# A two-layer transformer block on one core: another order of layer 1's steps

## What is computed

```python
# layer 0: full attention, 16 heads of 8; then 16 experts, one per token, and a shared one
h = layernorm(x) * (1 + ca) + sa
q, k, v = h @ Wq.T + bq, h @ Wk.T + bk, h @ Wv.T + bv
x = x + ga * (softmax(q @ k.T / sqrt(8)) @ v @ Wo.T + bo)
h = layernorm(x) * (1 + cb) + sb
scores = sigmoid(top1(h @ router_w.T))
gate, up = split(routed_in @ gate_up_proj[expert])
routed = (up * silu(gate)) @ down_proj[expert]
shared = silu(h @ shared_gate_w.T) * (h @ shared_up_w.T) @ shared_down_w.T
x = x + gb * (routed + shared)
# layer 1: causal attention, 8 query heads of 16 on one key and value head; then a token mix
h = layernorm(x) * (1 + ca) + sa
x = x + ga * (softmax(causal(q @ k.T * 128 ** -0.5)) @ v @ Wp + bp)
h = layernorm(x) * (1 + cb) + sb
r = sigmoid(mix_r(h) @ W_r.T); kk = square(relu(mix_k(h) @ W_k.T))
x = x + gb * r * (kk @ W_v.T)
```

## Time and profile before

| | us |
|---|---|
| median of 3 runs | 1134.35 (1130.43 to 1134.98) |
| the profiled execution | 1135.12 |
| its span, first to last instruction | 1133.3 |
| PE busy in the span | 1029.5 (91%) |
| DVE, ACT, POOL busy | 895.8, 821.1, 173.1 |
| mean granted TensorE clock | 0.952 |

### The profile page before, as it was taken

How to read it: one execution, slowest core, us unless ns; L and a number is a source line. 1 busy time by engine, 2 the same in 40 slices (tenths; PEclk the granted TensorE clock), 3 DMA queues, 4 the chain that set the end, 5 groups by cost and what they waited for, 6 DMA issues and landing times.

```text
span 1133.3 us, 22270 instructions
## 1 busy us (share of the span) xinstructions
PE 1029.5 (91%) x8778; PEld 356.0 (31%) x8778; DVE 895.8 (79%) x1131; ACT 821.1 (72%) x1585; POOL 173.1 (15%) x312
## 2 busy tenths in 40 slices
PE   4889999999999999999988998899978888798997
PEld 2332222222222222222222443343434453233314
DVE  5999999999999999999996776666756568587603
ACT  3239999998999989999875775467644555466675
POOL 4433200003000030000232002310221013000101
PEclk9569999999999999999998999899989999899987
DMA  3450511000000000000006221042003211200000
GB/s 108 128 142 7 136 30 29 2 2 2 2 2 2 2 2 1 2 2 2 2 19 188 61 72 36 13 95 49 2 1 112 82 52 30 36 10 2 11 1 10
DMA packets 47694, 42.08 MB, mean 37 GB/s; under 512 B 6534, under 2 KB 45798, under 8 KB 47590
## 3 DMA queue, kind: packets, MB, share of 16 engines
q1 hardware_dynamic: 45190, 35.17, 12.3%
q0 software_dynamic: 1824, 5.25, 1.6%
q10 hardware_dynamic: 576, 0.23, 0.1%
...
## 4 chain that ended last, share of the span: by engine, by line
PE 68%; DVE 17%; ACT 6%; issue 4%; DMA 2%; POOL 1%; SPq 1%; another core or an unknown queue 0%; DVEq 0%; POOLq 0%; ACTq 0%
PE O L936 24%; PE T L907 13%; DVE mx L1202 9%; PE S L866 8%; PE S L873 4%; ACT PT L1446 3%; PE T L916 3%; PE S L1047 2%; PE S L1015 1%; PE T L1055 1%; PE S L916 1%; PE T L945 1%; PE S L1005 1%; DVE Vf L1262 1%; DVE Vf L1266 1%
## 5 line engine op out<-in xcount | busy, mean ns | idle before, releaser
L1202 DVE TENSOR_REDUCE mx<-S 128x2 f32<-128x1024 f32 (+2 forms) x672 | 757.2, 1180 | 90.1 <-PE S L873 37.6
L1446 ACT ACTIVATE PT<-T 128x512 f32<-128x512 f32 (+2 forms) x1280 | 676.1, 580 | 111.5 <-PE T L907 40.1
L936 PE MATMUL O<-PT,Va 128*9 128x256 f32 (+1 forms) x4040 | 318.3, 387 | 3.3 <-ACT Os L1481 3.3
L866 PE MATMUL S<-Ks,Qs 48*128 48x512 bf16 x1024 | 206.3, 396 | 18.0 <-DVE mx L1202 9.6
L907 PE MATMUL T<-Qs,Ks 51*128 51x512 bf16 x1024 | 202.4, 388 | 13.1 <-ACT PT L1446 6.4
L907 PEld LDWEIGHTS T<-Qs,Ks 51*128 51x128 bf16 x1024 | 55.8, 93 | 223.3 <-issue 125.2
L936 PEld LDWEIGHTS O<-PT,Va 128*9 128x9 f32 x4040 | 60.0, 88 | 207.8 <-issue 198.3
L873 PE MATMUL S<-K,Qs 96*128 96x512 bf16 (+3 forms) x320 | 85.0, 356 | 14.9 <-DMA Qs<-rows_q 4.5
L916 PE MATMUL T<-Qs,K 99*128 99x512 bf16 (+3 forms) x256 | 72.2, 350 | 7.7 <-ACT PT L1446 4.0
L936 PE MATMUL O<-PT,V 128*17 128x512 f32 (+3 forms) x640 | 76.2, 549 | 0.0
L866 PEld LDWEIGHTS S<-Ks,Qs 48*128 48x128 bf16 x1024 | 52.5, 95 | 42.9 <-DVE mx L1202 28.4
...
## 6 DMA issues: line engine op xcount, KB each, us to landing
...
sorted_x<-XP POOLq DMA_DIRECT2D x1, 1792.0 KB, 10.7
```

Of the source, the lines that this page charges most:

```text
L866: m = e.matmul(two[:, i, :], Qs[r0:r0 + 48, hp, q0:q0 + 128], Ks[r0:r0 + 48, hp, CH * kb:CH * kb + CH], start=True, stop=True, tile_positi ...
L936: m = e.matmul(Ob[32 * g:32 * g + d1, lo:hi], v, PT[(2 * j + g // 2) % 4][:, p0 + lo:p0 + hi], start=(kt == 0 and halves[0] == 0), stop=Tr ...
L1202: e.tensor_reduce(mx[:, u % 2, h0:h0 + 2, kb], two[:, :, 0:n], AX.X, ALU.max).then_inc(free, 1)
L1446: e.activation(PT[(2 * j + pair) % 4][:, CH * i + lo:CH * i + CH], bank[:, lo:CH], ACT.Exp).then_inc(free, 1)
```

## The change

It changes only the order in which the plan lists its parts, and moves one norm from POOL to DVE.

1. **Score tiles apart.** In layer 1, a step's tiles were two before `st` half 1 and the rest before `pv`. Now one stands between the halves, one behind half 1, the rest behind `pv`. The lead is a table: units 0 to 4 still 3 steps, units 5 and 6 now 4, unit 7 now 5. `rate` counts a unit's tiles only once its chunk is ready (`may_begin`).
2. **Ranks.** `shared` for chunk 3 begins a step earlier, so that its first product `up` stands in front of `rank`.
3. **Experts.** In group 1 (chunk 3) a place of the book now holds `m0` of pair p and `m1` of pair p - 1, and the next place `m2` of pair p - 2. Before, `m0` and `m2` stood together, and `m1` in the next.
4. **Queries before keys**, in `rows`. For chunk 3 tiles may start 4 steps behind it, not 3. For chunks 0 to 2, `turn`, `rows` and `values` stand one step later.
5. **Sort.** `place` has six parts instead of five: the last one's first operation stays, its rest stands a step later, and the fetches half a step later.
6. `norm` of chunk 3 in stage 1 is done by DVE (L1146), not POOL (L1732).

```diff
-LEAD = (5, 3)
+LEAD = {(L, u): 5 if L == 0 or u == 7 else 4 if u > 4 else 3 for L, n in ((0, 16), (1, 8)) for u in range(n)}
...
-        for i in range(5):
-            at_side(s + 1 + i / 2, lambda i=i: P.stage("place", g, i))
+        for i, t in enumerate((1, 1.5, 2, 2.5, 3, 4)):
+            at_side(s + t, lambda i=i: P.stage("place", g, i))
...
         for p in range(n + 2):
-            at(s + int(pace * p), lambda p=p: first(p))
-            if 0 <= p - 1 < n:
-                at(s + int(pace * p), lambda p=p: between("m1", g, p - 1))
+            if g:
+                at(s + int(pace * p), lambda p=p: (m0(p), m1(p - 1)), lambda p=p: m2(p - 2))
+            else:
+                at(s + int(pace * p), lambda p=p: (m0(p), m2(p - 2)), lambda p=p: m1(p - 1))
...
         def rows():
-            project("k1", c, P.next_t())
-            project("q1", c, P.next_t())
-            split("k1", c, "dv")
-            split("q1", c, "dv")
+            for kind in ("q1", "k1"):
+                project(kind, c, P.next_t())
+            for kind in ("q1", "k1"):
+                split(kind, c, "dv")
             load_slabs()
-            ready[c] = now[0] + 3
+            ready[c] = now[0] + (4 if c == 3 else 3)
...
+        late = int(c < 3)
+        at(s + 2 + late, turn)
...
             route(t + 1, 3, 2)
+            shared(t + 5, 3, 1)
             s = sort(t + 5, 1)
-            shared(t + 6, 3, 1)
...
+    def may_begin(L, u):
+        return L == 0 or ready.get(UNITS[1][u][0], now[0] + 1) <= now[0]
...
-            due = sum(n for n, s0, (of, _) in zip(many, starts, units) if s0 - LEAD[of] <= J2)
+            due = sum(n for n, s0, of in zip(many, starts, units) if s0 - LEAD[of] <= J2 and may_begin(*of))
...
         else:
-            for _ in range(min(k, 2)):
+            if k:
                 emit_s()
             do_light(0.5)
             do_later()
             emit_st(J, 1)
-            for _ in range(k - 2):
+            if k > 1:
                 emit_s()
             if (L, u) >= (0, 15):
                 do_later()
             emit_pv(J - LAG, (0, 1))
+            for _ in range(k - 2):
+                emit_s()
```

More of the change, by code:

```diff
@@ L194, in sort @@
         for k in range(SLOTS[g]):
-            at_side(s + 4 + k / 2, lambda k=k: P.stage("fetch", g, k))
+            at_side(s + 4.5 + k / 2, lambda k=k: P.stage("fetch", g, k))
         s += 4 + (t1 - t0) // 2
@@ L201, in experts, with m0, m1, m2 @@
         n = GROUPS[g][3] // 2
-        def first(p):
+        def m0(p):
             if p < n:
                 beside("m0", g, p)
-            if 0 <= p - 2 < n:
-                beside("m2", g, p - 2)
-                for k in (2 * p - 4 + SLOTS[g], 2 * p - 3 + SLOTS[g]):
+        def m1(p):
+            if 0 <= p < n:
+                between("m1", g, p)
+        def m2(p):
+            if 0 <= p < n:
+                beside("m2", g, p)
+                for k in (2 * p + SLOTS[g], 2 * p + 1 + SLOTS[g]):
                     if k < GROUPS[g][3]:
@@ L245, in setup1 @@
         at_side(s + 1, lambda: P.norm(2, c))
-        at(s + 2, turn)
-        at(s + 3, rows)
-        at(s + 4, values)
+        late = int(c < 3)
+        at(s + 2 + late, turn)
+        at(s + 3 + late, rows)
+        at(s + 4 + late, values)
     def mix(s, c):
@@ L340, in may_score @@
             return False
-        L, u = tiles[si[0]][:2]
-        return L == 0 or ready.get(UNITS[1][u][0], now[0] + 1) <= now[0]
+        return may_begin(*tiles[si[0]][:2])
     def emit_s():
@@ L1140, in dv_program @@
                     if s == 1:
-                        continue
+                        if c < 3:
+                            continue
+                        dv.wait_ge(zero_x, 32)
                     dv.wait_ge(ln_scale[s], c + 1)
@@ L1302, in dv_program @@
                         e.tensor_copy(posu[:, t0:t1], posf[:, 0:nt]).then_inc(positions, 1)
-                    else:
+                    elif part == 4:
                         cm2 = kv[:, 0:16 * ni].rearrange("p (i n) -> p i n", i=ni)
@@ L1306, in dv_program @@
                                                 itf[:, 0:ni].unsqueeze(2).to_broadcast([128, ni, 16]), ALU.is_le))
+                    else:
+                        cm2 = kv[:, 0:16 * ni].rearrange("p (i n) -> p i n", i=ni)
                         dv.settle()
@@ L1727, in po_program @@
                     s, c = a
-                    if s == 1:
+                    if s == 1 and c < 3:
                         po.wait_ge(ln_scale[s], c + 1)
```

## The result

| | before | changed |
|---|---|---|
| median | 1132.39 us (1129.98 to 1134.98, 4 runs) | 1107.74 us (1105.72 to 1110.05, 4 runs) |
| the profiled execution's span | 1133.3 us | 1106.1 us |
| PE busy, idle in the span | 1029.5, 103.8 | 1017.8, 88.3 |
| mean granted clock | 0.952 | 0.967 |

The changed kernel takes 0.9776 of the time before (95% interval 0.9754 to 0.9797), 25 us less; between the two profiled executions it is 27.2 us, against the sum's 25.5. The forecast was 1110. That the total came so close is partly luck: D gave 7.1 us more than forecast, E, F and G together 6.3 less.

The account below looks back on a forecast made before the run. PE, busy 91% of the span, was taken as the bound, so only its waits and slow clock could be given back. Terms 1 + 0 + 7 + 7 + 0 + 4 + 2 + 4.5 = 25.5 us gave 1109.6, forecast 1110 (1103 to 1117).

Parts of the forecast that it names:

- D: Layer 1's window of the experts: shorter waits at m1, m2 and tiles, four tiles fewer; 7 us less (3 to 9).
- E: Layer 1's window around accept: DVE stands 3.7 us there, new PE wait 2.7 us; change 0 (-3 to +2).
- F: Layer 1's window of chunk 3's rows: wait and slow clock go, three-tile steps cost; 4 us less (0 to 6).
- G: Layer 1's window with unit 6's maxima: its 2.47 us wait mostly goes, three tiles fewer; 2 us less (0 to 3).
- A: Everything up to step 8: chunk 3's norm on DVE gives 1.0 us (0 to 1.1), the layers' seam 0.
- C: Layer 1's window with rank and the shared expert: waits and slow clock go; 7 us less (3.5 to 9).
- of 10.4 idle us I keep 5: Step in D: of the window's 10.4 us of idle PE time, 5 us was assumed to remain.
- halves too close: Rival: with one tile between the st halves, PE stops for ACT's bank in about 57 steps; 1141 us, chance 0.06.
- H: Layer 1's last window: unit 7's maxima come two steps earlier, the 2.70 us wait goes; 4.5 us less (1.5 to 5.1).
- Given back to DVE: Rival: DVE becomes the bound where tiles bunch, F gives nothing, accept costs 3, C and D give half; 1125 us, 0.17.
- The slow clock stays: Rival: waits vanish but the clock drops elsewhere, as behind accept; 1121 us, chance 0.13 for clock or DMA together.
- Not what it says: Rival: rank and chunk 3's rows are late anyway, C and F keep waits; 1121 us, 0.13 for clock or DMA together.

Follow-up runs that it names:

- The four kernels with the same tiles in D: The changed kernel, and it with the experts' old order, with tiles together in layer 1, and with both: 1107.74, 1111.38, 1119.93 and 1119.02 us.

## Why the prediction came out as it did, point by point

**What bounds.** Right: PE's work stayed and the gain was waits and clock. But the split of a window in busy and idle time hid a part. D's busy time fell by 4.9 us, and four tiles are 1.7 of it. The four kernels with the same tiles in D show the rest: idle 1.15, 5.2, 6.2 and 8.6 us, busy 43.96, 45.57, 45.56 and 46.17. With 4 to 5 us more of idle time come 1.6 us of busy time, with 7.5 come 2.2. So in these four kernels D grew by 1.3 to 1.4 us for each us of idle time; that it is because the products around a wait overlap less is argued, not shown.

**A.** Forecast -1.0 for the norm, 0 for the seam; measured +0.7. That figure says little: the same beginning came to step 8 anywhere between 827.6 and 835.9 us. What repeats is the piece from step 1 to step 8, and it is 1.9 us longer (24.32 against 22.38). Up to step 1 this pair of executions is 1.3 us shorter (803.56 against 804.85), with a granted clock from 700 to 760 us of 0.97 against 0.91. The step that failed is "the turn then finds its rows ready". They were ready (the turn, L835, has no wait), but DVE had the norm in its own queue, where it first waited 0.97 us for POOL's part of it. The division that frees the `st` bank (L1242) stood behind it, and PE waited 1.57 us there:

```profile
820.10 0.28 PE L929 MATMUL T<-Qs,K 99*128 99x256 bf16 x1 [1.57 <-DVE vw L1242]
```

```profile
817.71 1.11 DVE L1161 TENSOR_SCALAR XP<-xs,mv,rs 128x128 f32<-128x128 f32 x4 [0.97 <-POOL rs L1611]
818.74 0.68 DVE L1217 TENSOR_REDUCE mx<-S 128x2 f32<-128x512 f32 x1
819.34 0.24 DVE L1236 RECIPROCAL rl<-T 128x16 f32<-128x16 f32 x1
819.62 0.42 DVE L1242 TENSOR_TENSOR vw<-T,rl 128x256 f32<-128x256 f32 x1
```

The term measured 0.27 us with the tiles together and some 0.8 the other way with them apart. By the rule of the Trainium skill (Perfetto Trace Analysis, section Optimizing Scalar/DVE Operations), that such a move might not help, this term would be 0. The trace agrees in the result, but not on the ground of a shared port: DVE's norm took 1.11 us as in the earlier trace rows, and POOL was idle both times, so no run shows contention. What the rows show is DVE's queue. I also left out that tiles apart cost 1.15 us in steps 1 to 8 by themselves.

**C.** Right in size (-9.0 against -7, with two tiles more as counted), and clock 1.00 as forecast. The reason was half wrong: I gave the wait at `rank` to the `up` put in front of it. With the tiles apart alone the wait is 1.30 us, with the order of `rank` on top 0, and that order is worth 0.75 us.

**D.** The mis-sized term: -7 forecast, -14.1 measured. The step that failed is "of 10.4 idle us I keep 5". That is what one of the two parts does alone (6.2 or 5.2 left). I priced two parts that take different waits as one, and kept 5 us that nothing held. The busy time that went with the waits adds to it. The count of four tiles, 1.7 us, was right.

**E.** The chain was read rightly: 3.7 us of DVE at `accept` forecast, 4.0 measured; 2.7 us of PE, 1.8 measured. The slow stretch behind it, 1.8 us, I had left to a rival, and it came.

**F.** The wait of 4.48 us and its slow stretch went, and gave what was forecast: from step 32 to step 34 it is 8.2 us less (14.21 before, 6.06 now), of which four tiles moved away are 1.7, so 6.4 against 6.5. The term that was mis-sized is that of the tiles. Against the gain I set 1.5 us for steps bound by DVE and 1.3 for three tiles more, 2.8 together; it was 4.2. From step 34 to step 45 seven more tiles cost 5.9 us, 0.85 each. Steps 39 to 42, with three tiles each, take 14.19 / 4 = 3.55 us a step, which is DVE's 3 x 1.18. There the added tile costs what DVE needs beyond the old 2.82 us, 0.7 and not PE's 0.43. -2.2 instead of -4.

**G.** The wait went. But the rival *halves too close* was true in its mechanism, and I had it at 0.06. My working of it held an error: it let the second half's first product start and only its second wait. PE's program opens both banks of a half (`opened`, twice) ahead of its first product. With two tiles between, that product starts 1.31 us behind the first half's (1007.83 - 1006.52), so with one tile it would start some 0.44 earlier, 0.87 behind; but the exponential that frees the bank ends 0.98 us behind (1028.27 + 0.55 - 1027.84). So a stop was due in every step with two tiles and nothing else between, and it is seen: PE went on at 1029.01, 0.19 us behind that end. A stop of PE at the second half is also what the prediction named as its sign of being wrong, if it came throughout; it came in part of the steps. Its price was 0.29 us a step instead of 0.45 and more, and it did not count in all 57 steps: 3.0 us in G and 1.15 to 2.2 in steps 1 to 8, nothing in steps with three tiles, where DVE is the bound. I had put a mechanism that works by degrees among those that are so or not.

**H.** -5.0 against -4.5, of which 2.7 is the wait. The slow stretch was then worth 2.3 us; by the price in the Trainium skill (TensorE: Matmul & The Clock Gate, section Terms), half of 6.7, it would have been 3.4. The trace does not agree: the row decided rightly, and ACT is busy 28.7 of H's 32.4 us.

**The other rivals.** *Given back to DVE* is true of E and F, some 4 us, not of C and D. *The slow clock stays* came once, in E, at 1.8 us. *Not what it says* did not come.
